# Two chained convolutions on images of 192 x 192: a smaller edge exchange, summed bias weights, and a sequence of its own after the last sampling

## What is computed

```
x = x + L0(groupnorm(x))
x = x + L1(groupnorm(x))

L0: off = (sigmoid(conv3x3(x, w_off) + b_off) - 0.5) * 2   # two offsets, each below one pixel
    sampled = bilinear sample of every channel plane at (column - offx, row - offy)
    out = conv3x3(sampled, w_dcn) + b_dcn
L1: pooled = mean over the pixels
    kernels = relu(pooled @ w1 + b1) @ w2 + b2             # one 3x3 kernel per image and channel
    out = depthwise conv3x3(x, kernels)
```

## Time and profile before

| | us |
|---|---|
| median of 3 runs | 1601.03 (1600.81 to 1601.81) |
| the profiled execution's own time | 1599.84 |
| its span | 1598.0 |
| PE busy | 1509.8 (94% of the span) |
| DVE busy | 1362.4 (85%) |
| ACT busy | 1054.3 (66%) |
| POOL busy | 357.6 (22%) |

### The profile page before, as it was taken

How to read it: one execution, slowest core, us unless ns; L and a number is a source line. 1 busy time by engine, 2 the same in 40 slices (tenths; PEclk the granted TensorE clock), 3 DMA queues, 4 the chain that set the end, 5 groups by cost and what they waited for, 6 DMA issues and landing times.

```text
span 1598.0 us, 29952 instructions
## 1 busy us (share of the span) xinstructions
PE 1509.8 (94%) x12048; PEld 660.1 (41%) x12048; DVE 1362.4 (85%) x1264; ACT 1054.3 (66%) x1594; POOL 357.6 (22%) x382
## 2 busy tenths in 40 slices
PE   3778888999999999999999999999999999999888
PEld 1333334444444444444444444444444444444343
DVE  3999999999998998989989998899999999899800
ACT  4667566675777667775677757876687765655423
POOL 3000421205031230405121051302404041410010
PEclk9899999999999999999999999999999999999999
DMA  7365454765767567675667757676576665656446
GB/s 247 109 193 154 125 162 151 218 193 173 234 192 251 177 190 238 200 229 159 220 203 224 219 156 241 193 235 189 179 250 202 210 189 161 199 163 199 121 129 226
DMA packets 225274, 307.78 MB, mean 193 GB/s; under 512 B 16656, under 2 KB 167552, under 8 KB 225136
## 3 DMA queue, kind: packets, MB, share of 16 engines
q1 hardware_dynamic: 223632, 304.42, 61.8%
q0 software_dynamic: 1504, 1.45, 0.3%
HBM read 190.18 MB, written 38.14 MB: 143 GB/s over the span
## 4 chain that ended last, share of the span: by engine, by line
PE 65%; DVE 17%; ACT 7%; DMA 5%; issue 4%; SPq 2%; POOL 0%; DVEq 0%; ACTq 0%; POOLq 0%
PE z L357 31%; PE dc L397 16%; PE dw L427 12%; DMA st<-in_planes 3%; DVE nb L720 3%; DVE nb L717 3%; DVE nb L722 3%; PE dc L427 2%; DVE xv L710 2%; DVE nb L724 2%; DVE nb L726 2%; DVE nb L711 1%; DVE yr L743 1%; PE dc L401 1%; ACT dv L536 1%
## 5 line engine op out<-in xcount | busy, mean ns | idle before, releaser
L357 PE MATMUL z<-xv,wos 128*64 128x384 f32 x4608 | 764.3, 487 | 10.7 <-ACT du L536 10.7
L357 PEld LDWEIGHTS z<-xv,wos 128*64 128x64 f32 x4608 | 333.4, 136 | 424.6 <-issue 416.3
L397 PE MATMUL dc<-sr,wds 128*32 128x384 f32 x2304 | 438.3, 522 | 36.2 <-DVE yr L743 36.2
L397 PE MATMUL dc<-sh,wds 128*32 128x384 f32 x2112 | 396.6, 523 | 0.0
L703 DVE COPY_PREDICATED nb<-mu,xv 128x2280 f32<-128x2280 uint16 x96 | 271.2, 2825 | 32.8 <-ACT mu L543 32.4
L427 PE MATMUL dw<-yr,wy 128*64 128x388 f32 x672 | 250.7, 494 | 7.1 <-ACT ot L571 7.1
L427 PE MATMUL dw<-yh,wy 128*64 128x388 f32 x672 | 250.9, 494 | 0.0
L397 PEld LDWEIGHTS dc<-sr,wds 128*32 128x32 f32 x2304 | 134.0, 111 | 274.1 <-issue 273.9
L557 ACT ACTIVATE nb<-xv 128x2292 f32<-128x2292 f32 x96 | 203.0, 2114 | 0.4 <-DVE sr L731 0.4
L536 ACT ACTIVATE du<-z,ob 128x768 f32<-128x768 f32 x96 | 86.1, 897 | 154.9 <-PE z L357 151.3
L710 DVE COPY_PREDICATED xv<-mv,xv 128x768 f32<-128x768 uint16 x96 | 103.1, 1074 | 83.1 <-ACT mv L543 62.8
(11 more groups left out here) (118 smaller groups left out, 1615.7 us busy)
## 6 DMA issues: line engine op xcount, KB each, us to landing
xv<-in_x SPq DMA_DIRECT2D x272, 384.0 KB, 4.7
yr<-in_xr SPq DMA_DIRECT2D x96, 392.0 KB, 7.0
out<-ot SPq DMA_DIRECT2D x96, 388.0 KB, 5.4
yh<-yr SPq DMA_DIRECT2D x179, 196.0 KB, 5.0
st<-in_planes SPq DMA_DIRECT2D x56, 576.0 KB, 7.1
sh<-sr SPq DMA_DIRECT2D x160, 194.0 KB, 2.8
sh<-sr SPq DMA_DIRECT2D x32, 145.5 KB, 2.5
yr<-in_planes SPq DMA_DIRECT2D x8, 576.0 KB, 9.9
```

The lines of the kernel that those rows point to most:

```text
L357: last = nc.tensor.matmul(acc[m], weights[:, kx, :], view[:, :, kx:kx + W], start=kx == 0, stop=kx == 2)
L397: last = nc.tensor.matmul(dc[m, q, 0:NB * PAIRS], weights[:, kx, q], view[:, :, cols], start=first, stop=final)
```

## The change

The changed kernel does four things.

1. **Edge.** In an image's last chunk `deform` now runs the same 24 matmuls as elsewhere. Then six matmuls of one row block for each q, with weights `wde` (from the host, with signs) times the scale `rxs`, correct the row at the edge. Their input is a small tile `fe`, filled by a DMA of 32 partitions at the image's first chunk and one at its last. `s_shift` issues one DMA more at an image's first chunk and two more at its last.
2. **Bias weights.** POOL adds the three columns of the weights once at the start (`wo_sum`, `wd_sum`). `x_biases` then needs 4 and 8 matmuls, and multiplies with `mr`, mean times scale. POOL computes `mr` and `rxs` before the scaled weights `wos` and `wds`.
3. **After the last sampling.** The loops end at chunk 95, and each engine has a written sequence instead. DVE evacuates chunk 92 between picking and blending of chunk 95. PE runs two depthwise chunks in a row at some places. SP issues y_shift(n) ahead of store(n-3).
4. **Banks and slots.** From chunk 77 on `depthwise` uses the four banks of `z`, two for each chunk, and waits for `finish` of chunk n-2. The exchange of chunk 95 goes to the free tile `nb0`, so it does not need a slot of `yh`, and is issued right behind that of chunk 84.

```diff
-                            n3 = (NB - 1) * PAIRS
-                            nc.tensor.matmul(dc[m, q, 0:n3], weights[:, kx, q], view[:, 0:NB - 1, cols],
-                                             start=first, stop=False)
-
-                            nc.tensor.matmul(dc[m, q, n3:n3 + PAIRS], wde[:, 0, kx, q], view[:, NB - 1, cols],
-                                             start=False, stop=False)
-                            last = nc.tensor.matmul(dc[m, q, n3:n3 + PAIRS], wde[:, 1, kx, q],
-                                                    sh[:, SS * NB + b % 2, cols], start=False, stop=final)
+                            final = final and (r == 0 or j < CHUNKS - 1)
+                            last = nc.tensor.matmul(dc[m, q, 0:NB * PAIRS], weights[:, kx, q], view[:, :, cols],
+                                                    start=first, stop=final)
+                if j == CHUNKS - 1:
+                    n3 = (NB - 1) * PAIRS
+                    for kx in range(3):
+                        for h in range(2):
+                            m = slice(C * (2 + h), C * (2 + h) + C)
+                            last = nc.tensor.matmul(dc[m, q, n3:n3 + PAIRS], wde[:, kx, q],
+                                                    fe[:, b % 2, kx + h:kx + h + W - 1:2], start=False, stop=kx == 2)
...
                 if j == 0:
-                    sp.dma_start(sh[hi, SS * NB + b % 2, :], sr[lo, k, :]).then_inc(done, 16)
+                    sp.dma_start(se[hi, b % 2, :], sr[lo, k, :]).then_inc(se_in[b % 2], 16)
+                    sp.dma_start(fe[2 * C:3 * C, b % 2, :], sr[0:C, k, :]).then_inc(done, 16)
...
+                if j == CHUNKS - 1:
+                    sp.wait_ge(se_in[b % 2], 16 * (b // 2 + 1))
+                    sp.dma_start(sh[hi, k + NB - 1, :], se[hi, b % 2, :]).then_inc(done, 16)
+                    sp.dma_start(fe[C:2 * C, b % 2, :], sr[P - C:P, k + NB - 1, :]).then_inc(done, 16)
...
+        def late(n):
+            if n == LAST:
+                spare = nb[0][:].rearrange("p v k w -> p (v k w)")[:, 0:NB * Q * PW]
+                return spare.rearrange("p (k q w) -> p k q w", q=Q, w=PW)
+            return yh[:, h_at(n):h_at(n) + NB]
         def dw_bank(c, q):
-            return dc[:, q, 0:NB * OW] if last_image(c) else dw[:, 0:NB * OW]
+            return z[:, (c - TAIL) % 2, q, 0:NB * OW] if c >= TAIL else dw[:, 0:NB * OW]
...
-                if last_image(n):
-                    if n == TOTAL - CHUNKS:
-                        pe.wait_ge(y_done, Q * TOTAL)
-                    pe.wait_ge(o_done, Q * n + q - 1)
+                if n < TAIL:
+                    wait(pe, o_done, Q * n + q)
+                elif n < TAIL + 2:
+                    pe.wait_ge(z_read, 2 * LAST + n - TAIL + 1)
                 else:
-                    wait(pe, o_done, Q * n + q)
+                    pe.wait_ge(o_done, Q * (n - 2) + q + 1)
...
             def x_biases(b):
-                mean = nmx[b % 2][:]
+                mean = mr[b % 2][:]
                 for i in range(2):
-                    for kx in range(3):
-                        for m in halves:
-                            nc.tensor.matmul(sm[m, C_OB + i:C_OB + i + 1], wos[b % 2][:, i, kx], mean,
-                                             start=kx == 0, stop=kx == 2)
+                    for m in halves:
+                        nc.tensor.matmul(sm[m, C_OB + i:C_OB + i + 1], wo_sum[:, i], mean, start=True, stop=True)
...
+            depthwise_both(TAIL)
+            deform_both(LAST - 2)
+            depthwise_both(TAIL + 1)
+            depthwise_both(TAIL + 2)
+            deform_both(LAST - 1)
+            deform_both(LAST)
+            depthwise_both(TAIL + 3)
+            y_means(B - 1)
+            depthwise_both(TAIL + 4)
+            hidden(B - 1)
+            depthwise_both(TAIL + 5)
+            taps(B - 1)
+            depthwise_both(TAIL + 6)
+            y_bias(B - 1)
+            for n in range(TOTAL - CHUNKS, TOTAL):
+                depthwise_both(n)
...
+            for n in range(TAIL + 4, TOTAL - CHUNKS):
+                y_shift(n)
+                store(n - 3)
+            store(TOTAL - CHUNKS - 3)
+            y_shift(TOTAL - CHUNKS)
+            y_shift(LAST)
+            for n in range(TOTAL - CHUNKS + 1, LAST):
+                y_shift(n)
+                store(n - 3)
...
+            set_y_edges(B - 2)
+            y_norm(B - 1)
+            set_y_pads(B - 1)
+            y_weights(B - 1)
+            set_y_edges(B - 1)
```

More of the change, by code:

```diff
@@ L135, in block_kernel @@
         wo = sb("wo", [P, 2, 3, 2 * C])
+        wo_sum = sb("wo_sum", [P, 2, 2 * C])
+        wd_sum = sb("wd_sum", [P, Q, C])
+        mr = [sb(f"mr{s}", [P, 1]) for s in range(2)]
         wos = [sb(f"wos{s}", [P, 2, 3, 2 * C]) for s in range(2)]
@@ L330, in _ @@
             x_load(1)
-            for i in range(STEPS + 1):
+            for i in range(TOTAL):
                 b, o = divmod(i, CHUNKS)
@@ L344, in _ @@
                     st_load(b + 1, o)
-                if 0 <= i - DCN_STEP < TOTAL:
+                if 0 <= i - DCN_STEP:
                     residual(i - DCN_STEP)
+            y_shift(TAIL + 2)
+            residual(LAST - 2)
+            store(TAIL - 1)
+            residual(LAST - 1)
+            y_shift(TAIL + 3)
+            store(TAIL)
+            s_shift(LAST)
+            residual(LAST)
+            for n in range(TAIL + 4, TOTAL - CHUNKS):
[7 more added lines that the diff above has]
+                store(n - 3)
+            for n in range(LAST - 3, TOTAL):
+                store(n)
             for s in range(2):
@@ L496, in _ @@
             x_biases(0)
-            for i in range(STEPS):
+            for i in range(TOTAL):
                 b, o = divmod(i, CHUNKS)
                 c, d = i - DW_STEP, i - DCN_STEP
-                if 0 < b <= B and o == 7:
+                if b and o == 7:
                     y_bias(b - 1)
@@ L526, in _, with depthwise_both, deform_both @@
                         x_biases(b + 1)
+            def depthwise_both(n):
+                for q in range(Q):
+                    depthwise(n, q)
+            def deform_both(n):
+                for q in range(Q):
+                    deform(n, q)
+            depthwise_both(TAIL)
[14 more added lines that the diff above has]
+                depthwise_both(n)
         @block.scalar
@@ L756, in _ @@
                     accum_out=xs1[:, i:i + 1]).then_inc(first_sum, 1)
-            for i in range(STEPS):
-                if i < TOTAL:
-                    sample(i)
-                if 0 <= i - DCN_STEP < TOTAL:
+            for i in range(TOTAL - 1):
+                select(i)
+                blend(i)
+                if 0 <= i - DCN_STEP:
                     evacuate(i - DCN_STEP)
+            select(LAST)
+            evacuate(LAST - 3)
+            blend(LAST)
+            for n in range(LAST - 2, TOTAL):
+                evacuate(n)
         @block.gpsimd
@@ L925, in _ @@
             set_pads(0)
-            for i in range(STEPS):
+            for i in range(TOTAL):
                 b, o = divmod(i, CHUNKS)
-                if b < B and o == 0:
+                if o == 0:
                     if b == 0:
@@ L953, in _ @@
                     x_norm_var(b + 1)
-                if b < B and o == 10:
+                if o == 10:
                     set_pads(i + 1)
```

225 lines of the change are left out of this document (132 added, 93 removed).

## The result

The changed kernel takes **1571.37 us** (median of 4 runs, 1570.83 to 1572.4), the kernel before on the same chip 1600.92 (1599.07 to 1601.81): a ratio of 0.9823, 95% interval 0.981 to 0.9837. The forecast was 1574.2 with a range of 1565 to 1586. The span of the profiled execution is 1569.8 us where it was 1598.0: 28.2 less, forecast 26.8.

What follows compares the result with a forecast made beforehand. PE was taken to set the steady pace at 185.5 us an image, the DVE and ACT loop close behind at 183.1. Savings of 7.5 + 19.7 - 0.4 = 26.8 us gave a median of 1574.2, range 1565 to 1586.

Steps and rivals of the forecast that it cites:

- the 183.1 of DVE's loop: Second limit: the loop of DVE and ACT needs 183.1 us an image, only 2.4 less than PE takes.
- The prices of the edits: PE's image: edge deform 1.75 us shorter, x_biases 0.7 shorter, so 183.05 instead of 185.5.
- Half of PE's gain: Steady images: half of PE's 14.7 us gain counted, 1.25 an image or 7.5 us; bounds 0 and 14.7.
- SP's two added DMAs: Exchange at image's end: 0.46 to 0.6 us each to issue, ahead of the first statistics piece's load, which holds ACT.
- the first twenty steps: Early stretch: DVE's loop already rules there, so no gain was counted.
- The rival of the full gain: Steady images: PE's gain comes in full, 14.7 instead of 7.5 us, time 1567.0; chance 0.17.
- The tail: After the last sampling: span ends at 1578.3 instead of 1598.0, 19.7 us saved before 0.4 for late exchanges.
- The 0.4 for late transfers: Last twelve chunks: 0.4 us added for single late exchanges, at 294 GB/s with room up to 320.
- the slow clock for which I had put 1.3: Tail: PE's 2.8 us wait for the last exchange may bring the slow clock, costing 1.3, up to 2.1 us.
- The slow clock in every step: Rival, images: small PE gaps drop the clock once a step in 72 steps, 94 us more, about 1640; chance 0.04.
- `set_y_edges(6)`: Rival, tail: POOL's step waits for chunk 83's exchange, so the tail doesn't shorten, time 1593.5; chance 0.04.

Runs made afterwards that it cites:

- e5: e3 with the old bias matmuls in x_biases (36 matmuls) put back: 1564.3 us.
- e9: e8 with the edge deform and bias matmuls of the kernel before: 1563.42 us.
- e8: e3 with ACT's square of the evacuated chunk moved behind the mask mv: 1547.56 us.
- e3: The changed kernel with each statistics piece's load issued on SP ahead of that step's exchange and input load: 1560.58 us.
- e2: The changed kernel with the old loops, banks and slots after the last sampling, keeping the new edge and bias matmuls: 1591.72 us.
- e4: The changed kernel with DVE's evacuation of chunk 92 behind the blending of chunk 95, as before: 1576.14 us.
- e6: The changed kernel with SP issuing the exchange of chunk 95 late, behind that of chunk 94 and store(91): 1574.75 us.
- e7: The changed kernel with depthwise of chunks 77 to 83 in the single dw bank again: 1582.3 us.
- e10: The changed kernel with the two DMAs added to the exchange at an image's end issued behind the loads of x and first statistics piece: 1568.78 us.
- e1: The changed kernel with the old edge deform and bias matmuls, keeping the new sequences, banks and slots after the last sampling: 1580.14 us.
- e12: The kernel before with only the statistics' load moved ahead of the exchange: 1595.8 us.
- e11: The changed kernel with only ACT's square moved behind the mask mv, the statistics' load left in place: 1553.8 us.

## Why the prediction was right, point by point

**What bounds the kernel.** *Confirmed.* PE sets the pace in the images: an image gets 0.7 us longer when 0.7 us of matmuls are put back (e5), and e9 returns to 185.4. The number on which half of it turned, the 183.1 of DVE's loop, is also confirmed, by e8: with `mv` ahead of the square DVE's waits for it in the early stretch go from 10.0 us to nothing, and its twelve steps fall to 175.3. It stood so close to PE's new 183.0 that the changed kernel had no room for a late transfer.

**The prices of the edits.** An image's step with the edge went from 17.6 to 15.8 us between starts of L400, 1.75 to 1.8 saved; I said 1.75, from records of two column groups that overlap. In the new trace the records of L449 do come in pairs 0.01 us apart, one pair every 0.08 to 0.09 us. The step with `x_biases` went from 16.06 to 15.32, 0.74 for my 0.7. PE's image is 183.0 us in e3, where I had 183.05.

**Half of PE's gain.** L792 of chunk 95 starts at 1489.95 instead of 1496.54: 6.6 saved, forecast 7.5. That the size came so close is in part luck. The half was chosen between the bounds 0 and 14.7 and not worked out, and this time varies: in e2, e4, e6 and e7, whose lists are the same up to there, L792 of chunk 95 starts at 1489.89, 1487.67, 1486.81 and 1492.14. The five images of the trace average 184.5 us for my 184.3, but four of them are at 183.3 to 184.5, and the one of 187.5 makes up the rest. The waits came where I put them, DVE behind `mu`, ACT behind a late piece. What I saw less sharply is why the piece is late. I charged SP's two added DMAs with it; e10 moves those behind the load and gains little or nothing that can be told, while e3 takes the load out from behind SP's wait for the sampling, 7.7 us before the exchange instead of 4.2 after its start, and gains 10.8. The order on the queue decides more than two issues of 0.6 us. I had also counted nothing in the first twenty steps, where e3 gains 3.4 us and e8 16.3 by chunk 26. The rival of the full gain (1567.0) needed exactly this: e3 and e9 show that it was there to be had, 15.9 us for both edits where nothing else is in the way (my 14.7 and the deform of chunk 95, 1.75, make 16.45).

**The tail.** Measured from the start of L792 of chunk 95, so that the two traces can be laid over each other (forecast: the times of the text less 1496.5; measured: less 1489.95):

| | forecast | measured |
|---|---|---|
| deform(94) starts | 20.9 | 19.4 |
| deform(95) ends | 31.8 | 29.1 |
| mean read | 35.8 | 32.5 |
| `pooled` there | 38.4 | 35.1 |
| depthwise(84) starts | 46.6 | 43.5 |
| end of the span | 81.8 | 79.9 |

(The 0.4 for late transfers is not in the last row's forecast; with it the end is at 82.2.) By deform(95)'s end the forecast was 2.7 us too long. The exchange was in 1.5 us earlier than I had it: it was issued 15.4 us after L792 where I had 15.9, and all four DMAs were in 3.9 us later where I had 5.0. So PE waited 1.69 us instead of 2.8, and the slow clock for which I had put 1.3 did not come. (Its bound of 2.1 was also a little low: 4.6 us at half speed cost 2.3.) Behind that each step has my length to 0.6 us, until the last twelve chunks: 32.9 instead of 31.8, because PE waits 1.1 us for `yh<-yr` near 1540, where I had put 0.4 for transfers. The tail is 21.6 us shorter than it was, for a forecast of 19.3. Undone one by one, in the same measure: the order of the evacuation (e4) 6.8, the early last exchange (e6) 3.4, the banks (e7) 8.5, the edge (e1) 2.8. That makes 21.5 of 21.6 us, if they add up, which no run shows (by e8 and e9 the edge would be 2.0); the order of PE's chunks and of SP's list I didn't try one by one.

**The rivals.** The slow clock in every step did not come: in the images of e3, e8 and e11 PE is busy without a hole at a clock of 1.00. The Trainium skill (TensorE: Matmul & The Clock Gate, "HAM oscillation") describes it for loops whose every turn has a gap; no run here had such a loop in the images. The early stretch is one, and there the trace agrees in part: PE idles 22 us in its twelve steps, and the clock falls in five of them, those in which it waits longest (2.73 to 3.39 us, where the other waits are of 0.46 to 1.74). In 140.2 to 143.4, 170.9 to 174.2, 201.7 to 204.9, 232.4 to 235.6 and 276.8 to 283.4 us of the changed kernel the granted clock was 0.50. What that costs where DVE sets the pace no run separates. The time that I gave this rival does not follow from its terms: 72 falls of 1.3 us are 94 us, and with the forecast of 1574.2 that is 1668, not 1640. `set_y_edges(6)` held nothing up: the read of the mean at 1522.48 is followed by POOL 0.07 us later. The transfers did not bind either, beyond the 1.1 us that PE waited near 1540: the window of the last chunks has the engines 0.86 busy at 277 GB/s.

So the sum was 26.8, the span fell by 28.2: 0.9 too much in the steady part, 2.3 too little in the tail.

## What to carry to other kernels

Look for the second limit before you shorten the first, and for what eats the distance between them: here the two were 0.1 us an image apart after the change, and a single load in the wrong place of a queue cost 7 us that it had not cost before (10.8 in e3, 3.6 in e12). A load that depends on nothing should not stand behind a queue's wait for a computation. And one instruction moved behind a few others on ACT (e11), far from any change made, gave 17.6 us: where a loop over two engines sets the pace, ask which result the other engine waits for and issue that first.

## What I had not expected of the hardware

PE's clock fell after some idle stretches and not after others: after 2.20 us at chunk 49 the next 2.7 us ran at 0.50, after 6.92 us in e4 the next 3.7 us, and after 3.51 in e6 the next 2.7; after 1.69 us in the changed kernel it stayed at 1.00. Where ten waits of PE for `finish`, up to 2.1 us long, stood within 88 us (e7), it stayed at 1.00 too. The length of the wait alone does not decide it: in e3 PE waited 3.38 us before 275.23 and the next 4.7 us ran at 1.00, and it waited only 2.24 us before 290.24 and ran at 0.50 behind it.
